# An attention stage's probabilities times values: float32 products in place of float16 parts

## What is computed

```python
def step(carry, qkv):
    M, z = carry
    q, k, v = qkv
    sq = _sigma(q)
    denom_q = jnp.sum(sq * z[:, :, None, :], axis=-1, keepdims=True) + EPS
    A_mem = jnp.matmul(sq, M) / denom_q
    scores = jnp.matmul(q, jnp.swapaxes(k, -2, -1)) * inv_sqrt_dk
    scores = jnp.where(causal, -jnp.inf, scores)
    A_dot = jnp.matmul(jax.nn.softmax(scores, axis=-1), v)
    A_s = beta * A_mem + (1.0 - beta) * A_dot
    ...
    return ((M_new, z_new), A_s)
```

## Time and profile before

| | us |
|---|---|
| median of three runs | 1305.98 |
| the three runs | 1304.98, 1312.92, 1305.98 |
| the profiled execution | 1306.74 |
| its span in the profile | 1304.9 |

### The profile page before, as it was taken

How to read it: one execution, slowest core, us unless ns; L and a number is a source line. 1 busy time by engine, 2 the same in 40 slices (tenths; PEclk the granted TensorE clock), 3 DMA queues, 4 the chain that set the end, 5 groups by cost and what they waited for, 6 DMA issues and landing times. The chain is left out here.

```text
span 1304.9 us, 53730 instructions
## 1 busy us (share of the span) xinstructions
PE 1160.5 (89%) x19576; PEld 983.5 (75%) x19576; DVE 906.2 (69%) x2481; ACT 706.5 (54%) x1393; POOL 941.2 (72%) x989
## 2 busy tenths in 40 slices
PE   4689999999899899999723799999999999999995
PEld 1477777888777777777513588888888888888884
DVE  2589999999998999989888545444444544444542
ACT  2377888888888888878634133233333323333331
POOL 3168999999998989989841466666676666767653
PEclk8599999999999999989755899999999999999998
DMA  8323343334333433433445676777878787777770
GB/s 217 84 68 80 105 127 113 95 105 118 103 109 97 115 102 101 116 96 109 112 96 169 127 136 129 145 130 125 130 142 136 130 144 123 138 138 139 136 110 1
DMA packets 203977, 153.09 MB, mean 117 GB/s; under 512 B 103930, under 2 KB 181842, under 8 KB 203602
## 3 DMA queue, kind: packets, MB, share of 16 engines
q1 hardware_dynamic: 163042, 81.90, 25.4%
q0 software_dynamic: 32592, 56.75, 25.2%
q10 hardware_dynamic: 8096, 11.01, 3.1%
HBM read 63.58 MB, written 44.04 MB: 82 GB/s over the span
## 5 line engine op out<-in xcount | busy, mean ns | idle before, releaser
L1289 PE MATMUL psum<-xT,xall 128*128 128x256 f16 x3408 | 385.3, 273 | 13.5 <-DMA xT<-grow 13.3
L1289 PEld LDWEIGHTS psum<-xT,xall 128*128 x3408 | 334.1, 98 | 53.6 <-issue 14.1
L1349 POOL DMA_INDIRECT out<-late,sidx x142 | 230.7, 1625 | 160.1 <-DVE late L1340 99.4
L1297 ACT ACTIVATE sg<-psum 128x512 f32<-128x512 f32 x142 | 84.6, 596 | 282.7 <-PE psum L1289 204.2
L1302 DVE SCALAR_TENSOR_TENSOR late<-psum,sg 128x512 f32<-128x512 f32 x142 | 98.2, 691 | 171.3 <-ACT sg L1297 118.1
L1269 POOL DMA_INDIRECT grow<-moe_rows,gidx x142 | 150.5, 1060 | 86.1 <-DVE sidx L1155 43.1
L1323 PE MATMUL psum<-w2s,hT 128*128 x1704 | 199.3, 274 | 3.8 <-DVE w2s L1375 3.5
L1323 PEld LDWEIGHTS psum<-w2s,hT 128*128 128x128 f16 x1704 | 167.4, 98 | 24.3 <-issue 4.3
L1313 DVE TENSOR_TENSOR hT<-late,hT 128x512 f16<-128x512 f32 x142 | 98.8, 696 | 98.8 <-ACT hT L1309 84.2
L1309 ACT ACTIVATE hT<-late 128x512 f16<-128x512 f32 x142 | 89.4, 629 | 113.7 <-DVE late L1302 98.5
L673 POOL TENSOR_TENSOR pT<-sc,pT 128x1024 f16<-128x1024 f32 x64 | 136.6, 2134 | 10.5 <-ACT pT L669 10.3
(11 more groups left out here) (255 smaller groups left out, 2300.9 us busy)
## 6 DMA issues: line engine op xcount, KB each, us to landing
stk<-qk SPq DMA_DIRECT2D x384, 64.0 KB, 2.8
moe_rows<-hrows SPq DMA_DIRECT2D x128, 128.0 KB, 3.0
out<-xall SPq DMA_DIRECT2D x128, 64.0 KB, 2.5
raw<-in_w ACTq DMA_DIRECT2D x26, 256.0 KB, 3.1
xall<-in_x ACTq DMA_DIRECT2D x16, 256.0 KB, 4.0
raw<-in_w SPq DMA_DIRECT2D x8, 512.0 KB, 9.5
xall<-in_x SPq DMA_DIRECT2D x8, 384.0 KB, 8.2
grow<-moe_rows,gidx POOLq DMA_INDIRECT x142
```

Of the source, the lines that this page charges most:

```text
L1289: i = k.e.matmul(bank[:, n * LONG:(n + 1) * LONG], w13s[:, bass.ds(ex_reg * (G * 4 * I) + ((2 * c + b_) * 2 * I + col), P)], xT[:, k.x, a, ...
L1297: done(k.e.activation(sg[:, half, :], bGate[half][:, :], ACT.Silu, scale=1.0 / W_SCALE), "sg")
L1349: k.e.indirect_dma_start(out_rows, bass.IndirectOffsetOnAxis(ap=sidx[:, n:n + 1], axis=0), yo[:, k.v, q, :], None, bounds_check=B * T - 1, ...
```

## The change

- `p_high`, `p_rest` and `v_rest` go, with their semaphores `phi`, `plo` and `vlo` and the tile `pT`. `x_load` now hangs behind `softmax_exp`.
- The values stay float32 (`v_high`), each head with a column of ones of its own: 17 columns.
- `pv` multiplies the float32 exponentials in `sc` by them: 16 heads times 2 batches, 32 products of 64 partitions by 64 columns of weights and 17 moving columns. Batch 0 reads partitions 0 to 63 and writes partitions 0 to 63 of `bkD`, batch 1 the other halves; `bkE` is not written any more by this stage.
- So tokens lie on the partitions as in `att_o`: `pv_dve` is one product of 128 x 256, `pv_den` one of 128 x 16 as before, `inv_om` has a column per head.
- `softmax_exp` waits for `pv` of two tiles before (the buffer `sc`), `pv` for `softmax_exp` and `v_high`.

```diff
-VW = 2 * DK + 1
+VW = DK + 1
...
-    inv_om = sb("inv_om", [P, NPAIR])
+    inv_om = sb("inv_om", [P, H])
...
-    vs = sb("vs", [P, 4, 2, NPAIR, VW], F16)
+    vs = sb("vs", [P, 4, H, VW])
...
-            e.memset(vs[:, b_, 0, :, 2 * DK:VW], 1.0).then_inc(s_c, 1)
-            e.memset(vs[:, b_, 1, :, 2 * DK:VW], 0.0).then_inc(s_c, 1)
+            e.memset(vs[:, b_, :, DK:VW], 1.0).then_inc(s_c, 1)
...
-        pair = btile2[:, :].rearrange("p (n two) -> p two n", two=2)
-        for par in range(2):
-            rows = slice(par * SEG, (par + 1) * SEG)
-            e.tensor_scalar(inv_om[rows, :], pair[rows, par, :], 1.0, 1.0 / A_SCALE, ALU.add, ALU.mult).then_inc(s_gb, 1)
+        e.tensor_scalar(inv_om[:, :], btile2[:, :], 1.0, 1.0 / A_SCALE, ALU.add, ALU.mult).then_inc(s_gb, 1)
...
-    pT = sb("pT", [P, 2, 2, 8, P], F16)
-    rr = sb("rr", [P, 2, 2, NPAIR])
+    rr = sb("rr", [P, 2, H])
...
     def v_high(k):
...
-        k.wait("vlo", 4)
-        done(k.e.activation(vs[:, k.j, 0, :, 0:2 * DK], bkC[:, 0:D].rearrange("p (n w) -> p n w", w=2 * DK),
+        done(k.e.activation(vs[:, k.j, :, 0:DK], bkC[:, 0:D].rearrange("p (h w) -> p h w", w=DK),
...
-    def v_rest(k):
-        k.wait("vhi")
-        k.wait("PV", 4)
-        done(k.e.scalar_tensor_tensor(out=vs[:, k.j, 1, :, 0:2 * DK], in0=bkC[:, 0:D].rearrange("p (n w) -> p n w", w=2 * DK),
-                                      scalar=1.0 / W_SCALE, in1=vs[:, k.j, 0, :, 0:2 * DK], op0=ALU.mult,
-                                      op1=ALU.subtract), "vlo")
...
     def softmax_exp(k):
         k.wait("sT")
-        k.wait("plo", 2)
-        k.wait("phi", 2)
+        k.wait("PV", 2)
...
-    def p_high(k):
-        k.wait("exp")
-        k.wait("PV", 2)
-        k.wait("plo", 2)
-        done(k.e.activation(pT[:, k.b, 0, :, :].rearrange("p n t -> p (n t)"), sc[:, k.b, :], ACT.Copy), "phi")
-    def p_rest(k):
-        k.wait("phi")
-        k.wait("PV", 2)
-        done(k.e.tensor_tensor(pT[:, k.b, 1, :, :].rearrange("p n t -> p (n t)"), sc[:, k.b, :],
-                               pT[:, k.b, 0, :, :].rearrange("p n t -> p (n t)"), ALU.subtract), "plo")
...
     def pv(k):
-        k.wait("plo")
-        k.wait("phi")
-        k.wait("vlo")
+        k.wait("exp")
+        k.wait("vhi")
         k.wait_banks("PV")
         for half in range(2):
             for gu in range(4):
-                pair = (gu // 2) * 4 + half * 2 + gu % 2
-                for a, b_ in PARTS:
-                    for r, bank in zip(HALVES, (bkD, bkE)):
-                        i = k.e.matmul(bank[:, pair * VW:(pair + 1) * VW], pT[r, k.b, a, half * 4 + gu, :],
-                                       vs[r, k.j, b_, pair, :], start=((a, b_) == PARTS[0]),
-                                       stop=((a, b_) == PARTS[-1]))
+                for m in range(2):
+                    h = ((gu // 2) * 4 + half * 2 + gu % 2) * 2 + m
+                    at = (half * 4 + gu) * P + m * SEG
+                    for r in HALVES:
+                        i = k.e.matmul(bkD[r, h * VW:(h + 1) * VW], sc[r, k.b, at:at + SEG], vs[r, k.j, h, :],
+                                       start=True, stop=True, skip_group_check=True)
         done(i, "PV")
+    def found_heads():
+        return bkD[:, 0:H * VW].rearrange("p (h w) -> p h w", w=VW)
     def pv_den(k):
         k.wait("PV")
...
-        done(k.e.tensor_tensor(rr[:, k.b, :, :],
-                               bkDE[:, :, 0:NPAIR * VW].rearrange("p b (n w) -> p b n w", w=VW)[:, :, :, 2 * DK],
-                               bc_mid(inv_om[:, :], 2), ALU.mult), "pdn")
+        done(k.e.tensor_tensor(rr[:, k.b, :], found_heads()[:, :, DK], inv_om[:, :], ALU.mult), "pdn")
     def pv_scale(k):
...
-        done(k.e.reciprocal(rr[:, k.b, :, :], rr[:, k.b, :, :]), "rcp")
+        done(k.e.reciprocal(rr[:, k.b, :], rr[:, k.b, :]), "rcp")
     def pv_dve(k):
-        de = [bank[:, 0:NPAIR * VW].rearrange("p (n w) -> p n w", w=VW) for bank in (bkD, bkE)]
         k.wait("rcp")
...
-        for b2 in range(2):
-            for par in range(2):
-                r = slice(par * SEG, (par + 1) * SEG)
-                i = k.e.tensor_tensor(
-                    att_o[b2 * SEG:(b2 + 1) * SEG, k.b, :].rearrange(
-                        "p (n w) -> p n w", w=2 * DK)[:, :, par * DK:(par + 1) * DK],
-                    de[b2][r, :, par * DK:(par + 1) * DK], bc(rr[r, k.b, b2, :], DK), ALU.mult)
-        done(i, "ado")
+        done(k.e.tensor_tensor(att_o[:, k.b, :].rearrange("p (h w) -> p h w", w=DK), found_heads()[:, :, 0:DK],
+                               bc(rr[:, k.b, :], DK), ALU.mult), "ado")
...
-        "vector": [(2, aggr), (9, mem_a), (9, mem_v), (0, stats), (9, v_rest), (9, v_new), (11, pv_den),
+        "vector": [(2, aggr), (9, mem_a), (9, mem_v), (0, stats), (9, v_new), (11, pv_den),
...
-                  (8, softmax_exp), (8, p_high), (5, h1t), (12, ln2_act), (17, logit_copy), (6, sk_act),
+                  (8, softmax_exp), (5, h1t), (12, ln2_act), (17, logit_copy), (6, sk_act),
...
-        "gpsimd": [(12, p_rest), (8, ln_mult), (16, ln2_mult), (17, rows_lo), (15, ln2_scale), (12, update_add),
+        "gpsimd": [(8, ln_mult), (16, ln2_mult), (17, rows_lo), (15, ln2_scale), (12, update_add),
...
-    chunk_work = {p_high: x_load, logit_copy: early_exp, ln2_shift: choice_a, resid: choice_b, var_eps2: choice_c,
+    chunk_work = {softmax_exp: x_load, logit_copy: early_exp, ln2_shift: choice_a, resid: choice_b, var_eps2: choice_c,
...
```

More of the change, by code:

```diff
@@ L406, in attention @@
     h2T = sb("h2T", [P, 2, 2, G, P], F16)
-    names = ("stats aggr eps pow nmr xn lna T1 h1T h1L pqk pv qkh exq rel vhi vlo qlo sig scr mx mTr mTh mTl "
-             "sT exp phi plo memm den rec mV mA vpr skt upm umul madd PV pdn rcp ado aadd ahi alo AT aT Wo "
+    names = ("stats aggr eps pow nmr xn lna T1 h1T h1L pqk pv qkh exq rel vhi qlo sig scr mx mTr mTh mTl "
+             "sT exp memm den rec mV mA vpr skt upm umul madd PV pdn rcp ado aadd ahi alo AT aT Wo "
              "gat res st2 ag2 ep2 pw2 nm2 xn2 l2a l2b hhi hlo h2Tr h2T rtr lg").split()
@@ L423, in attention @@
         "pv": ((("umul", 2),),
-             (("vhi", 1), ("vlo", 1), ("vpr", 1),)),
+             (("vhi", 1), ("vpr", 1),)),
         "pqk": ((("umul", 3),),
@@ L438, in attention @@
              (("mTh", 1), ("mTl", 1), ("mx", 1),)),
-        "upm": ((("qlo", -2), ("rel", -2), ("qkh", -2), ("sig", -2), ("vhi", -1), ("vlo", -1), ("vpr", -1),),
+        "upm": ((("qlo", -2), ("rel", -2), ("qkh", -2), ("sig", -2), ("vhi", -1), ("vpr", -1),),
              (("umul", 1),)),
```

## The result

| | kernel before | changed kernel |
|---|---|---|
| median, us | 1305.48 (1301.61 to 1312.92, 4 runs) | 1331.43 (1328.81 to 1333.73, 4 runs) |
| ratio | | 1.0184, 95% interval 1.0149 to 1.0219 |
| span of the profiled execution | 1304.9 | 1331.8 |
| attention stage in it, first to last tile's product | 574.4 | 601.8 |

The change costs 1.8%, where a gain of 0.7% was forecast; the time lies above the range. Outside the stage nothing moved: the spans differ by 26.9 us, the stages by 27.4. (In the changed kernel the product is L730; the lines behind the edit are 5 to 31 lower.)

The account below looks back on a forecast made before the run. PE and DVE were full side by side, leaving PE the bound: 63 x 8.72 = 549.4 us, plus DMA waits 11.4, L75 2, clock 5, gives 567.8 against 574.4; less 2.8 for POOL waits, 1297.3 us in all, range 1281 to 1313.

Parts of the forecast that it names:

- There are 16 steps: The new product group on PE: 16 steps of 0.055 us, 1.04 us against 0.71, so +0.33 us a tile.
- rival 3: Product group on PE: four passes per float32 product make it 1.76 us, 1343 us in all; chance 0.03.
- if the two quarters do not run side by side at all: Upper bound for the new product group on PE: 32 steps in series, 1.92 us (+1.21 a tile).
- rivals 2: Product group on PE is longer than its loads: 1309 us by L729's step, 1353 with quarters in series; chance 0.09.
- L621's step: Low end for the new product group on PE, at the float16 step of L621: 0.64 us (-0.07 a tile).
- DMA waits, L75 and the clock: Losses kept in the attention stage: stacking DMA waits 11.4 us, DVE's early expert weights 2 us, slow clock 5 us.
- L753's waits for POOL: Attention stage: the old product's waits for POOL go with POOL's part in it, -2.8 us.
- the cut of DVE's work: DVE's round in the attention stage falls by 1.23 us to 7.4 us, 1.3 us below PE's.
- rival 4: Attention stage: the clock falls more often because half the array idles 1 us a round, 1328 us; chance 0.03.
- the likeliest case: Whole kernel: a small gain, 1293 to 1303 us, chance 0.40.
- rival 1: Attention stage: all unevenness goes and PE runs at 8.72 us a round throughout, 1279 us; 0.33 given to below 1293.

Follow-up runs that it names:

- e4_load: Changed kernel with the removed roundings, remainders and four-piece scaling put back beside the products, which wait for them but do not read them: 1339.84 us, ratio 1.0257.
- e1_half: Changed kernel with 16 products a tile instead of 32, 34 moving columns each, the odd heads' probabilities left out: 1278.61 us, ratio 0.9798.
- e2_block: Changed kernel's result from 16 products with both batches' keys on 128 weight rows, block-diagonal values, DVE's four pieces back: 1286.55 us, ratio 0.9872.
- e3_f16: Changed kernel with exponentials and values in float16, their rounding remainders left out: 1275.81 us (one run).

## Why the prediction was wrong

**The step that failed: "There are 16 steps".** The price of a step was right (0.055 predicted, 0.058 measured); there are 32 of them. 32 x 0.055 + 0.16 = 1.92 us, and 1.97 was measured. I had the proof in the earlier trace rows and read past it: L729 shows x16 records, and I wrote "16 products in four quarters, so 4 steps". Its code has three loops of two, so 8 products:

```python
        for g in range(G):
            for hh, lanes in enumerate(HALVES):
                for r, bank in zip(HALVES, (bkB, bkC)):
                    i = k.e.matmul(bank[lanes, g * MW:(g + 1) * MW], ...
```

L683 likewise shows x32 for 16 products. So a count such as x16 is one of records: one for a float16 product, two for a float32 one. Counted in records, four quarters take four at once, and my steps of 0.067 and 0.086 us are near for these lines: the single starts give 0.059 us a step of 68 moving columns and 0.113 us a step of 132. But then the new group must be counted in records too: 32 products are 64 records, two at once, 32 steps. I counted records on one side and products on the other. L753's x48, which I checked against `pv`'s 48 products, is float16 and gave no warning.

**Four passes (rival 3) were set aside on the same miscount.** I wrote that L729 "would need 4 x 0.10 + 0.16 = 0.56 us at least and takes 0.43". With its 8 products that is 2 steps, 0.36 us: the row did not speak against the rule. Its group of 1.76 us (1343 us in all) and the bound "if the two quarters do not run side by side at all" (1.92 us) came nearest to the measured one, and rivals 2 and 3 had 0.12 between them. That they lie near is luck: the quarters do run side by side, and what sets the step is two records a product, paid by their weight loads.

The four passes themselves are there, though they set no price here. The set-up has 6 float32 products of 512 moving columns (L364), again in two records each, 12 in all. Its last five records in the kernel before, and L809's 6 float16 products of 256 columns, with the start of what follows (granted clock 1.00 in both places):

```profile
16.86 2.31 PE L364 MATMUL psum<-wmod_sb,cs 128*8 128x512 f32 x5
...
312.10 0.82 PE L809 MATMUL psum<-wo,aT 128*128 128x256 f16 x6
312.76 0.27 PE L538 MATMUL psum<-idf,h 128*128 128x128 f32 x1
```

A single record of L364 is 0.59 us long, so the five start (2.31 - 0.59) / 4 = 0.43 us apart. L809 steps by 0.66 / 6 = 0.11 us, so 512 float16 columns would take 0.22. A float32 record thus takes twice the time per moving column, and the two records of a product four times. The Trainium skill's page "FP8 and Floating Point Precision" (section "TensorE Precision Notes") says 4 passes for true FP32, and here the trace agrees. The prediction's "The trace does not agree" came of the miscount. By the same rate 17 columns take 17 x 0.43 / 512 = 0.014 us (an estimate), 34 columns 0.029, both well under the load's 0.058; which fits that they cost the same.

**The sum, term by term.** The stage was forecast at 567.8 - 2.8 = 565.0 us and took 601.8, 36.8 more. (The sum for L621's step has a slip of no account: 16 x 0.031 + 0.16 is 0.66 us, not 0.64.)
- The group: 63 x (1.97 - 1.04) = +58.6.
- What was kept for DMA waits, L75 and the clock, 18.4 us, was not lost: -18.4. At the longer round the DMA's waits are 2.8 us and DVE has 2 us to spare for L75; the second part's rounds, at a mean clock of 0.98, are 315.1 / 33 = 9.55 us long, the first's, at 1.00, 286.7 / 30 = 9.56.
- The 2.8 us that I took off as L753's waits for POOL belong to the same unevenness and were counted in it: +2.8.
- The rest: PE's round without the group was 8.39 - 0.71 = 7.68 us and is 601.8 / 63 - 1.97 = 7.58: 63 x -0.10 = -6.2, with the waits that remain in it.

**What held.** PE is the bound and DVE waits for it; the cut of DVE's work is 1.2 us a round; POOL's and ACT's work is off the path at a round of 9.6 us (e4_load); the clock does not fall more often with half the array idle (rival 4: 1.00 and 0.98 after, 1.00 and 0.96 before).

**The second error.** e1_half shows that the likeliest case would have been wrong with the group as predicted, too: 1279 us, rival 1, which had 0.33. By my sum its stage is 63 x (7.68 + 1.06) + 18.4 - 2.8 = 566.2 us; it took 549.2. Of the 17.0 us between, 6.3 are again the rest of PE's round, 0.10 us shorter than I read off one quiet round. The other 10.7 were kept for waits and clock: the clock's 5 us were not lost, and of the DMA's waits, which the weight loads still show, the stage shows some 4.9 us (549.2 - 63 x 8.64, a round taken from the changed kernel's average).

**The range.** It left out the serial group (1.92 us), a bound of my own, as worth less than 2 in 10 on the strength of a row whose count I had not checked against the code.

## What to carry to other kernels

Before a duration is divided by a count from a trace, check that count against the loops of the code, at least once for each data type: a float32 product stands there twice, with two weight loads. For float32 products with few moving columns count weight loads and their columns: fill the 128 rows (here with zeros: e2_block, whose stage is 42 us shorter than the changed kernel's) rather than issue more products or wider ones. Where one engine takes over as the only bound, the waits of the others mostly go; where its round then gets shorter, look at once for the chain that is next, here the stacking DMAs on SP, worth 23 us at a PE round of 8.2 us, some 5 to 7 at 8.6 and 4 where DVE was full as well.

## What the runs showed of the hardware

- A float32 product is two matmul records and two weight loads (4096 for 64 x 32 products), a float16 product one (2048 in e3_f16). A float32 transposition is one (128 of L538 in the kernel before, two a tile).
- A step of two float32 loads side by side is 0.058 us for 64 columns, with 64 rows or 128, and 0.111 us for 128 columns; in float16 it is 0.031 us for 64 columns and 0.025 us for 128.
- 17 or 34 moving columns under such a load cost the same: two float32 records with 34 columns step at the pace of two with 17. Four records side by side with 68 columns step at 0.059 us, with 132 at 0.113 (L683 of the kernel before).
- Where the columns set the time, a float32 record takes 0.43 us for 512 moving columns (L364), float16 0.11 us for 256 (L809): four times as long for a product.
